# Causal mask of a self-attention stage: 512 mask products on TensorE replaced by 128 selections on GpSimd

## The reference

```
x = _layernorm(x + _L0_attn_ref(x, ...))
...
qkv = x @ w_in.T + b_in
q, k, v = jnp.split(qkv, 3, axis=-1)          # then 16 heads of 16
scores = einsum('bhqd,bhkd->bhqk', q * 0.25, k) + causal_bias   # -inf for keys behind the query
attn = softmax(scores, axis=-1)
out = einsum('bhqk,bhkd->bhqd', attn, v)       # then @ w_out.T + b_out
```

## Time and profile before

| what | value |
|---|---|
| median of 3 runs | 2307.2 us (2304.66 to 2307.98) |
| the profiled execution | 2305.3 us, of it a span of 2303.5 us |
| PE busy | 1997.3 us (87%) |
| DVE busy | 1437.4 us (62%) |
| ACT busy | 1205.6 us (52%) |
| POOL busy | 726.2 us (32%) |

### The profile page before, as it was taken

One profiled execution on the slowest core, in us unless ns is written; L12 is line 12 of the kernel. 1 busy time (PEld: TensorE's weight loads), 2 busy tenths in 40 slices (PEclk: granted clock), 3 DMA queues, 4 the chain that ended last, 5 costly groups with the idle time before them and its releaser, 6 DMA issues. The chain is left out here.

```text
span 2303.5 us, 32739 instructions
## 1 busy us (share of the span) xinstructions
PE 1997.3 (87%) x11274; PEld 1117.9 (49%) x11274; DVE 1437.4 (62%) x2698; ACT 1205.6 (52%) x2758; POOL 726.2 (32%) x1040
## 2 busy tenths in 40 slices
PE   6899999999896699999999886979899967798886
PEld 3344444444342455565555554656566643344444
DVE  5665675676772465656888975576744344567645
ACT  2355655655554375566877760758532324364352
POOL 4261221220000200212553551585652322343323
PEclk8899999999999799999999998989999978899898
DMA  7536444444511200001011105100011256554421
GB/s 157 119 64 150 93 85 90 90 84 76 77 49 29 77 1 8 29 26 38 35 53 44 44 35 189 42 8 28 9 33 50 63 119 119 122 105 94 81 63 39
DMA packets 134470, 156.56 MB, mean 68 GB/s; under 512 B 38445, under 2 KB 104881, under 8 KB 134210
## 3 DMA queue, kind: packets, MB, share of 16 engines
q1 hardware_dynamic: 134306, 154.48, 29.4%
HBM read 99.16 MB, written 46.86 MB: 63 GB/s over the span
## 5 line engine op out<-in xcount | busy, mean ns | idle before, releaser
L733 DVE TENSOR_REDUCE negm_sb<-psA 128x1 f32<-128x640 f32 (+6 forms) x352 | 351.1, 1026 | 182.0 <-PE psA L407 175.6
L545 ACT ACTIVATE pbuf_sb<-psB 128x512 f32<-128x512 f32 (+1 forms) x608 | 329.7, 573 | 227.1 <-PE psB L419 198.6
L1273 ACT ACTIVATE pw_sb<-psA,nmx_sb 128x154 f32<-128x154 f32 x512 | 192.3, 390 | 133.5 <-DVE nmx_sb L1418 133.5
L416 PE MATMUL psB<-qst_sb,kst_sb 99*128 99x512 bf16 (+3 forms) x768 | 234.4, 334 | 19.8 <-issue 7.8
L405 PE MATMUL psA<-kst_sb,qst_sb 96*128 96x512 bf16 (+3 forms) x768 | 195.2, 330 | 7.6 <-DVE negm_sb L733 5.7
L1418 DVE TENSOR_REDUCE nmx_sb<-psA 128x4 f32<-128x616 f32 x128 | 101.9, 796 | 124.9 <-PE psA L1042 124.5
L433 PE MATMUL psO<-pbuf_sb,V_sb 128*32 128x512 f32 (+3 forms) x1536 | 162.6, 503 | 4.4 <-ACT OT_sb L531 2.2
L416 PEld LDWEIGHTS psB<-qst_sb,kst_sb 99*128 99x128 bf16 x768 | 74.9, 98 | 181.0 <-ACT pbuf_sb L545 128.1
L2950 DVE TENSOR_REDUCE negm_sb<-psA 128x2 f32<-128x320 f32 x256 | 115.7, 480 | 66.6 <-PE psA L2713 65.2
L2833 ACT ACTIVATE pb_sb<-psB 128x512 f32<-128x512 f32 x160 | 93.4, 601 | 119.4 <-PE psB L2723 114.3
L2713 PE MATMUL psA<-kst_sb,qst_sb 97*128 97x160 bf16 x512 | 82.9, 250 | 45.5 <-DVE negm_sb L2950 39.6
(11 more groups left out here) (306 smaller groups left out, 4213.9 us busy)
## 6 DMA issues: line engine op xcount, KB each, us to landing
qst_sb<-parts_dram SPq DMA_DIRECT2D x192, 128.0 KB, 4.7
parts_dram<-parts_sb SPq DMA_DIRECT2D x32, 384.0 KB, 2.6
kst_sb<-parts_dram SPq DMA_DIRECT2D x96, 128.0 KB, 7.7
OTC_sb<-OT_sb SPq DMA_DIRECT2D x128, 64.0 KB, 6.1
rden_sb<-dens_dram SPq DMA_DIRECT2D x128, 64.0 KB, 2.2
x_dram<-X_sb SPq DMA_DIRECT2D x64, 128.0 KB, 1.7
y_dram<-yw_sb SPq DMA_DIRECT2D x16, 512.0 KB, 2.8
Y_sb<-y_dram SPq DMA_DIRECT2D x16, 512.0 KB, 9.0
```

The source lines that it names most:

```text
L416: last = nc.tensor.matmul(psB[:, k, at:at + hi - lo], kst[0:MAX_ROWS, gg % 3, h, i * P:(i + 1) * P], qst[0:MAX_ROWS, gg % 3, h, lo:hi], st ...
L545: nc.scalar.activation(pbuf[:, key % 2, heads[0]:heads[-1] + 1, lo:hi], psB[:, (nb.n - 1) % 2, 0:len(heads) * (hi - lo)] .rearrange("p (h ...
L733: nc.vector.tensor_reduce(out=negm[:, gg % 2, heads[0]:heads[-1] + 1, j], in_=psA[:, (na.n - 1) % 2, :].rearrange("p (h n) -> p h n", h=le ...
L1273: last = nc.scalar.activation(pw[:, m % 2, h, :], psA[:, m % 2, at:at + K], ACT.Exp, bias=nmx[:, m % 2, h:h + 1], accum_out=psx[:, m % 3, ...
```

## The change

In the second score pass the mask product goes. POOL gets `clear_future(s)` in its place: once the exponentials of the diagonal tile of unit s are there, one `affine_select` over 128 partitions x 4 heads x 128 columns of `pbuf` writes 0 where the query lies before the key. The product with V over the half of the queries that holds the diagonal waits for it on a new semaphore, `future_cleared`.

In POOL's list the select of unit k - 10 stands ahead of `split_qk(k)`, but behind the quantiser, `scale_values` and `inverse_deviation`. `scale_values` comes at `early_groups(k - 6)` in place of k - 5 and as four pieces of 256 columns. The quantiser's six steps are cut into four pieces each, two pieces a step. The layernorm's late parts move a step: `inverse_deviation` to k + 1, `normalise` on DVE to k + 2, `store_tile` on SP to k + 3. On PE, `values` for the second half of the queries moves from behind the step's first piece of scores to behind its second piece, when the unit before had key 4 to 7.

```diff
+    future_cleared = sem0("f_future_cleared")
+    def diagonal_exps(s):
+        i = KEY_ORDER[s % 8]
+        before = 8 + sum((len(second_units(KEY_ORDER[(k - LEAD) % 8])) if k >= LEAD else 0) + bool(qk_unit(k))
+                         for k in range(s + LEAD))
+        return before + sum(lo == i * P for _, lo, _ in second_units(i))
...
-                sp.wait_ge(quantised, 2)
+                sp.wait_ge(quantised, 8)
...
-                if k >= 2 and out_unit(k - 2):
-                    store_tile(*out_unit(k - 2))
+                if k >= 3 and out_unit(k - 3):
+                    store_tile(*out_unit(k - 3))
...
-                                            qst[0:MAX_ROWS, gg % 3, h, lo:hi], start=True, stop=not diagonal)
-                    if diagonal:
-                        last = nc.tensor.matmul(psB[:, k, at:at + P], identb[:, :], maskl[:, :], start=False, stop=True)
+                                            qst[0:MAX_ROWS, gg % 3, h, lo:hi], start=True, stop=True)
...
                 pe.wait_ge(b_free, seen)
+                if c == i // 4:
+                    pe.wait_ge(future_cleared, 8 * gg + KEY_ORDER.index(i) + 1)
...
-                    if u == 0 and s >= 1:
+                    if u == (KEY_ORDER[(s - 1) % 8] >= 4) and s >= 1:
                         values((s - 1) // 8, KEY_ORDER[(s - 1) % 8], exps_at[s - 1], 1)
...
-                nc.gpsimd.tensor_tensor(OTC[:, pair % OCN, :], OTC[:, pair % OCN, :], rden[:, :], ALU.mult).then_inc(ot_scaled, 1)
+                for n in range(4):
+                    at = slice(n * 256, (n + 1) * 256)
+                    last = nc.gpsimd.tensor_tensor(OTC[:, pair % OCN, at], OTC[:, pair % OCN, at], rden[:, at], ALU.mult)
+                last.then_inc(ot_scaled, 1)
...
+            def clear_future(s):
+                key = KEY_ORDER[s % 8]
+                pool.wait_ge(b_free, diagonal_exps(s))
+                nc.gpsimd.affine_select(out=pbuf[:, key % 2, :, key * P:(key + 1) * P],
+                                        in_=pbuf[:, key % 2, :, key * P:(key + 1) * P], compare_op=ALU.is_ge, fill=0.0,
+                                        base=0, pattern=[[0, 4], [1, P]], channel_multiplier=-1).then_inc(future_cleared, 1)
...
             for k in range(LAST + 1):
+                if 18 <= k < 30:
+                    for piece in (0, 1) if k % 2 == 0 else (2, 3):
+                        quantise((k - 18) // 2, piece)
+                done = early_groups(k - 6)
+                if done is not None and done % 2 == 1:
+                    scale_values(done // 2)
+                if k >= 1 and out_unit(k - 1):
+                    inverse_deviation(*out_unit(k - 1))
+                if LEAD <= k < LAST:
+                    clear_future(k - LEAD)
                 if qk_unit(k):
                     split_qk(*qk_unit(k))
-                if 18 <= k < 30 and k % 2 == 0:
-                    quantise((k - 18) // 2)
-                done = early_groups(k - 5)
-                if done is not None and done % 2 == 1:
-                    scale_values(done // 2)
-                if out_unit(k):
-                    inverse_deviation(*out_unit(k))
...
-                if k >= 1 and out_unit(k - 1):
-                    normalise(*out_unit(k - 1))
+                if k >= 2 and out_unit(k - 2):
+                    normalise(*out_unit(k - 2))
```

More of the change, by code:

```diff
@@ L127, in decoder_kernel @@
     masku = sb("masku", [P, P], BF16, first_stage)
-    maskl = sb("maskl", [P, P], BF16, first_stage)
     qst = sb("qst", [P, 3, 4, S], BF16, first_stage)
@@ L414, in second_scores @@
                 for a, h in enumerate(heads):
-                    at, diagonal = a * (hi - lo), lo == i * P
+                    at = a * (hi - lo)
                     last = nc.tensor.matmul(psB[:, k, at:at + hi - lo], kst[0:MAX_ROWS, gg % 3, h, i * P:(i + 1) * P],
-                                            qst[0:MAX_ROWS, gg % 3, h, lo:hi], start=True, stop=not diagonal)
-                    if diagonal:
-                        last = nc.tensor.matmul(psB[:, k, at:at + P], identb[:, :], maskl[:, :], start=False, stop=True)
+                                            qst[0:MAX_ROWS, gg % 3, h, lo:hi], start=True, stop=True)
                 last.then_inc(b_full, 1)
@@ L590, in inverse_deviation @@
                 nc.gpsimd.tensor_tensor(rstd[:, j:j + 1], std[:, j:j + 1], mhalf[:, :], ALU.pow).then_inc(rstd_ready, 1)
+            def clear_future(s):
[4 more added lines that the diff above has]
+                                        base=0, pattern=[[0, 4], [1, P]], channel_multiplier=-1).then_inc(future_cleared, 1)
             link(nc.gpsimd.memset(ones[:, :], 1.0))
             link(nc.gpsimd.memset(mhalf[:, :], -0.5))
-            for m in (ident, identb, masku, maskl):
+            for m in (ident, identb, masku):
                 link(nc.gpsimd.memset(m[:, :], 0.0))
@@ L600, in _ @@
                                          base=0, pattern=[[-1, P]], channel_multiplier=1))
-            link(nc.gpsimd.affine_select(out=maskl[:, :], in_=maskl[:, :], compare_op=ALU.is_ge, fill=MASKED,
-                                         base=0, pattern=[[1, P]], channel_multiplier=-1))
             link(nc.gpsimd.memset(V[:, :, :, 0:H * (HD + 1)].rearrange("p a j (h e) -> p (a j) h e", h=H)[:, :, :, HD:HD + 1], 1.0))
@@ L611, in _, with quantise @@
                         rest_of(u)
-            def quantise(step):
+            def quantise(step, piece):
                 i = step // 3
                 raw = (w_raw1, w_raw2)[i]
+                dst = (w1q, w2q)[i][:, :, :].rearrange("p c n -> p (c n)")
                 if i == 0:
                     raw = raw.rearrange("p c n -> p (c n)")
-                if step == 0:
+                if step == 0 and piece == 0:
                     pool.wait_ge(m1_ready, 1)
+                part = slice(piece * 512, (piece + 1) * 512)
@@ L621, in quantise @@
                 if step % 3 == 0:
-                    link(nc.gpsimd.tensor_scalar(raw, raw, rs1[:, i:i + 1], ROUND, ALU.mult, ALU.add))
+                    link(nc.gpsimd.tensor_scalar(raw[:, part], raw[:, part], rs1[:, i:i + 1], ROUND, ALU.mult, ALU.add))
                 if step % 3 == 1:
-                    link(nc.gpsimd.tensor_scalar(raw, raw, ROUND, 1.0, ALU.subtract, ALU.min))
+                    link(nc.gpsimd.tensor_scalar(raw[:, part], raw[:, part], ROUND, 1.0, ALU.subtract, ALU.min))
@@ L625, in quantise @@
                 if step % 3 == 2:
-                    nc.gpsimd.tensor_scalar((w1q, w2q)[i][:, :, :].rearrange("p c n -> p (c n)"), raw, -1.0, None,
-                                            ALU.max).then_inc(quantised, 1)
-                    pool.wait_ge(quantised, i + 1)
+                    nc.gpsimd.tensor_scalar(dst[:, part], raw[:, part], -1.0, None, ALU.max).then_inc(quantised, 1)
+                    pool.wait_ge(quantised, 4 * i + piece + 1)
             for k in range(LAST + 1):
+                if 18 <= k < 30:
+                    for piece in (0, 1) if k % 2 == 0 else (2, 3):
+                        quantise((k - 18) // 2, piece)
```

## The result

The changed kernel takes 2343.9 us, the median of 4 runs (2340.36 to 2347.84). The kernel before took 2305.93 us in the 4 runs beside it. The ratio is 1.0166, with a 95% interval of 1.0141 to 1.0192: slower by some 38 us. The prediction was 2344, with a range of 2316 to 2366.

The account below looks back on a forecast made before the run. PE sets the pace in the first stage's loop, busy 624 of 697 us. Terms +29.3 - 1.7 + 7.5 + 4.8 - 6 x 0.9 + 0.8 + 1.3 = +36.6 on 2305.3 give 2341.9, so 2344 against run medians; range 2316 to 2366.

Parts of the forecast that it names:

- The shared wait: POOL's select queues behind scale_values, which waits for the inverses; PE waits in seven places: 35.6 us, 29.3 after sooner transposes.
- the 0.25 that masks behind it give back: Mask products of keys 2 to 0 behind the shared wait give back 0.25 us each: -1.7 us.
- the clock: PE's granted clock falls behind the new long waits: 6.9 us at k = 49, 81, 97, 0.6 at k = 33 and 129; +7.5.
- the 1.3: In the last ten steps ACT sets the pace and the select is on the path, 0.74 us at the end: +1.3 us.
- sooner transpose: Less PE work precedes the transpose, so DVE's maximum is made 0.9 us sooner, seven times, taken off the shared wait.
- -5.4: Plain cycles lose mask products from PE's path: 0.9 us saved in each of 6 cycles.
- +0.8: The quantiser's pieces on POOL, in 12 steps, delay selects of light steps once: +0.8 us.
- Behind `split_qk`: split_qk, 3.0 us on POOL, delays the next step's select: 1.5 us after key 7, 0.4 after key 5; +4.8 us.
- The mask products: Of 29.7 us for 512 products, about half shorten PE's cycle: 0.9 us a cycle, the others fall into ACT's bursts.
- The select: POOL's select takes 0.61 us; slack at key 5 is 0.6 us, key 4 is level, so 0 us in plain cycles.
- The rest: Layernorm parts a step later and SP's store wait: hidden, 0; SP's wait for quantised pieces over before k = 31.

Follow-up runs that it names:

- select first: The changed kernel with clear_future moved to the head of POOL's step: 2309.8 us, ratio 1.0012 to the kernel before.
- without mask products: The kernel before without the 512 mask products of the second pass and with no select in their place: 2301.4 us, ratio 0.9971.
- two selects: Each select made twice, in the kernel of all together with the late weights at k = 33: 2308.9 us, ratio 1.0006 to the kernel before.
- everything behind the select: The select first kernel with split_qk behind the next step's select and scale_values a step later (k - 7): 2304.3 us, ratio 0.9981.
- inverses sooner: SyncE sends the inverses at k - 3, ahead of the maxima: changed kernel 2313.0 us, ratio 1.0017; kernel before 2305.9 us, ratio 0.9979.
- all together: Changed kernel with select first, split_qk and scale_values (k - 6) behind it, inverses at k - 3, late weights at k = 36: 2298.2 us, ratio 0.9961.

## Why the prediction was right

**The shared wait** was the step that carried it. Seven places, each in key 3's step: predicted resume at landing + 3.86 us, seen 209.31 - 205.69 = 3.62. The pieces took 2.76 us in all (0.722 each, no gap) where I took 3.12, the select 0.634 for 0.61, and the steps from POOL to PE and between POOL's items 0.09 us more than I had. The edits at either end of the chain confirm the cause: moving the select ahead of the wait took some 35 us off, and moving the transfer ahead of the wait, with POOL's list untouched, left some 5 us of the 38, once the late weights were out of the way.

**The sum, cycle by cycle.** A cycle runs from one transpose of the maxima to the next, in PE's timelines of both kernels. The forecast of a cycle is its terms of the sum: the shared wait, the 0.25 that masks behind it give back, the clock, and for the last cycle the 1.3. The others have -6.3 (sooner transpose), +4.8, -5.4 and +0.8.

| cycle from the transpose at | forecast, us | before, us | changed, us | added, us |
|---|---|---|---|---|
| k = 32 | 3.65 | 41.59 | 45.38 | 3.79 |
| k = 48 | 6.65 | 42.83 | 50.22 | 7.39 |
| k = 64 | 3.65 | 44.82 | 45.40 | 0.58 |
| k = 80 | 6.65 | 43.20 | 47.97 | 4.77 |
| k = 96 | 9.30 | 33.94 | 40.39 | 6.45 |
| k = 112 | 4.35 | 44.71 | 49.17 | 4.46 |
| k = 128, to the stage's end | 8.45 | 71.25 | 85.36 | 14.11 |
| all the others together | -6.1 | | | -4.75 |
| sum | 36.6 | | | 36.80 |

That the sum came within 0.2 us is partly luck. The mechanism, the places and the size of the waits are right, but the last cycle was 5.7 us too low, and those from k = 64, 80 and 96 were 1.9 to 3.1 too high.

**The clock** is the term that was mis-sized, by where it falls. For k = 129 I took 0.3 us (0.6 with k = 33), as ACT would set the pace there. The four steps behind that wait took 4.9 us more at a granted clock of 0.65. Not all of it may belong to the long wait: the clock was down ahead of it, and without mask products and without a long wait the same four steps ran at 0.56. With the select first, too, the stretch from the last transpose to the last product with V ran at 0.76 (42.75 us), in the kernel before at 1.00 (35.42). Low stretches followed all seven long waits. The Trainium skill, TensorE: Matmul & The Clock Gate, Part 1, says that the throttled rate is the default and activity releases it. By that rule each long wait is followed by a slow stretch, and the runs agree: seven of seven. Taking (1 - clock) x length over the seven windows gives 16 us against the 4.6 of the earlier trace rows. That is a bound on what they cost, as not every such stretch is on the path.

**Sooner transpose.** I took 0.9 us. From the 16 products with V in the step of key 7 to the transpose it took 577.58 - 572.42 = 5.16 us before and 598.17 - 593.71 = 4.46 in the changed kernel, so 0.7.

**Behind `split_qk`.** All five waits stand after key 7, 1.2 us each for the 1.5 I took. Two of them (286.43 and 469.46) stand ahead of a long wait that covers them, as written. Those after key 5, for which I took 0.4 each, did not show.

**The mask products.** The sum counts 8.0 us for them, and some 3 more inside the sooner transposes. By the kernel without them they were worth 12.3 us up to the last transpose, so the term was about right. That the whole run shows only 6.7 comes from the 8.1 us lost behind, at the low clock. The cycles are not alike. A plain one is 0.6 us shorter for the 0.9, by the bursts of ACT that I had named:

```profile
568.45 3.36 ACT L545 ACTIVATE pbuf_sb<-psB 128x512 f32<-128x512 f32 x6 [1.05 <-PE psB L419]
601.88 3.36 ACT L545 ACTIVATE pbuf_sb<-psB 128x512 f32<-128x512 f32 x6 [1.06 <-PE psB L419]
...
589.80 4.02 ACT L552 ACTIVATE pbuf_sb<-psB 128x512 f32<-128x512 f32 x7 [1.00 <-PE psB L423]
622.59 4.09 ACT L552 ACTIVATE pbuf_sb<-psB 128x512 f32<-128x512 f32 x7 [1.00 <-PE psB L423]
```

33.43 us apart before (the first two rows) and 32.79 after. The cycles from the transposes at k = 56, 88 and 120 are 1.9 us shorter each.

**The select.** It took 0.634 us. The 769 ns for 512 elements of the Trainium skill, GPSIMD Engine Reference, section 3.1, lie above that; the measurement decides. Its slack was read too high at key 5 (0.6, measured 0.2 with two selects) and right at key 4 (level). With one select of 0.63 us nothing hung on it.

**The rest.** The weights' wait for the quantiser cost nothing in the change, as written (183.02 for 182.15). At the end two waits of 0.46 and 1.54 us stand for the 1.3.

## What to carry to other kernels

When work is moved to an idle engine, read its list, not its load: the selects took 81 us on an engine that was idle for 560 of 697, and the change cost 38 us, some 35 of them since one item ahead of a select waits for a transfer. Find where that transfer lands against the step in which the new work is wanted; moving the waiting item later does nothing if the landing is later still. And before a saving on the busiest engine is counted, follow the chains that pass by it (here maxima out to memory and back): they take back a part of the saving, here 3.9 us of longer waits. And read the granted clock of the stretches that the change leaves with less to do: a saving can be lost there, as 8.1 us were without the mask products.

## What the runs showed that was not expected

- The one-time load of 3 MB with its 13 issues, 7 to 12 us of SyncE's queue, held up the maxima once in each of five kernels: PE waited 3.8 us (select first), 4.0 (all behind), 9.7 and 9.5 (inverses sooner, changed kernel and kernel before) and 7.4 (all together). Moving the load to k = 33 took the waits of 9.7, 9.5 and 7.4 away.
- From the last transpose to the last product with V, PE's granted clock was 1.00 in the kernel before and with everything behind the select (35.42 and 35.55 us). It was 0.76 with the select first (42.75 us), 0.65 without mask products (43.44) and 0.67 in the changed kernel (48.68), and only the last of these has a long wait there. What decides it was not tested.
- PE's clock was at 0.50 for 4.6 us behind a wait of only 1.20 us at 424.5 and at 0.63 behind one of 1.19 at 120.4, while behind a wait of the same length at 244.2 it was 1.00. What told them apart was not tested.
- The select of 128x512 took 634 ns, close to a cast of the same size (611). With the 293 ns of 128 bf16 columns an estimate is (634 - 293) / 384 = 0.89 ns for each further column.
